# A graph network on one core: two middle biases moved from TensorE to VectorE, score rows carried through memory, leak by two exponentials, new queue orders

## Reference

```python
h = jnp.maximum(_layernorm(x), 0.0);  x = x + L0(h, adj)   # hypergraph convolution, 256 -> 512 -> 256
h = jnp.maximum(_layernorm(x), 0.0);  x = x + L1(h, adj)   # tanh(norm(A) @ h @ W + b)
h = jnp.maximum(_layernorm(x), 0.0);  x = x + L2(h, adj)   # attention, below
h = jnp.maximum(_layernorm(x), 0.0);  x = x + L3(h, adj)   # three graph layers, two with relu
# L2:
y = x @ w;  s = y @ a
A = s[..., :, None] + s[..., None, :]
A = jnp.tanh(A / 8.0) * 8.0
A = jnp.where(A >= 0, A, 0.1 * A)
A = jnp.exp(A) * A_shape
A = A / jnp.sum(A, axis=-1, keepdims=True) * jnp.sum(A_shape, axis=-1, keepdims=True)
out = A @ x @ w
# L3, twice with relu and once without:
x = jax.nn.relu(jnp.einsum('bnm,bmh->bnh', adj, x @ W1) + b1)
```

## Time and profile before

| | before |
|---|---|
| time, median of 3 runs | 1438.51 us (1437.08 to 1438.55) |
| the profiled execution | 1435.79 us, span of its trace 1433.8 us |
| TensorE busy | 1392.3 us, 97%, x10900 |
| TensorE weight loads | 1331.7 us, 93% |
| VectorE busy | 1287.9 us, 90%, x4001 |
| ScalarE busy | 990.5 us, 69% |
| GpSimd busy | 947.7 us, 66% |
| DMA | 62.70 MB, mean 44 GB/s |

### The profile page before, as it was taken

How to read it: one execution, slowest core, us unless ns; L and a number is a source line. 1 busy time by engine, 2 the same in 40 slices (tenths; PEclk the granted TensorE clock), 3 DMA queues, 4 the chain that set the end, 5 groups by cost and what they waited for, 6 DMA issues and landing times.

```text
span 1433.8 us, 34585 instructions
## 1 busy us (share of the span) xinstructions
PE 1392.3 (97%) x10900; PEld 1331.7 (93%) x10900; DVE 1287.9 (90%) x4001; ACT 990.5 (69%) x2312; POOL 947.7 (66%) x1876
## 2 busy tenths in 40 slices
PE   3799999999999999999999999999999999999997
PEld 2799999999999999999999999999999999999996
DVE  5789999999999999999999999999999999999984
ACT  3577777777777777777777777777777777777763
...
DMA packets 83078, 62.70 MB, mean 44 GB/s; under 512 B 40304, under 2 KB 65520, under 8 KB 83056
## 3 DMA queue, kind: packets, MB, share of 16 engines
...
...
## 4 chain that ended last, share of the span: by engine, by line
PE 95%; DVE 2%; ACT 1%; issue 0%; DMA 0%; POOL 0%; SPq 0%; DVEq 0%; POOLq 0%
PE BANK L365 29%; PE BANK L330 24%; PE BANK L372 15%; PE WIDE L365 8%; PE WIDE L341 8%; PE WIDE L372 4%; PE BANK L357 2%; PE BANK L315 2%; PE BANK L384 2%; DMA TMP_D<-in_l2wt 0%; PE WIDE L278 0%; DVE BN_B L550 0%; DVE BN_C L550 0%; ACT UHI_D L444 0%; PE WIDE L284 0%
## 5 line engine op out<-in xcount | busy, mean ns | idle before, releaser
L444 ACT ACTIVATE UHI_B<-BANK 128x512 fp32r<-128x512 f32 x96 | 57.0, 593 | 43.9 <-PE BANK L330 43.9
L444 ACT ACTIVATE UHI_D<-BANK 128x512 fp32r<-128x512 f32 x96 | 57.1, 595 | 41.1 <-PE BANK L330 41.1
L444 ACT ACTIVATE UHI_C<-BANK 128x512 fp32r<-128x512 f32 x96 | 57.0, 594 | 41.0 <-PE BANK L330 41.0
L444 ACT ACTIVATE UHI_A<-BANK 128x512 fp32r<-128x512 f32 x96 | 57.1, 594 | 39.1 <-PE BANK L330 39.1
L599 DVE TENSOR_TENSOR ULO_D<-BANK,UHI_D 128x512 fp32r<-128x512 f32 x96 | 65.2, 680 | 18.7 <-ACT UHI_D L444 18.0
L732 POOL TENSOR_TENSOR LN_A<-MV_A,EPS 128x2 f32<-128x2 f32 x80 | 15.9, 198 | 92.3 <-DVE MV_A L558 92.3
L599 DVE TENSOR_TENSOR ULO_A<-BANK,UHI_A 128x512 fp32r<-128x512 f32 x96 | 65.2, 680 | 12.3 <-ACT UHI_A L444 11.8
L599 DVE TENSOR_TENSOR ULO_C<-BANK,UHI_C 128x512 fp32r<-128x512 f32 x96 | 65.1, 678 | 11.1 <-ACT UHI_C L444 9.3
L599 DVE TENSOR_TENSOR ULO_B<-BANK,UHI_B 128x512 fp32r<-128x512 f32 x96 | 65.7, 684 | 10.4 <-ACT UHI_B L444 8.5
L732 POOL TENSOR_TENSOR LN_D<-MV_D,EPS 128x2 f32<-128x2 f32 x80 | 15.8, 197 | 84.7 <-DVE MV_D L558 84.7
L732 POOL TENSOR_TENSOR LN_B<-MV_B,EPS 128x2 f32<-128x2 f32 x80 | 16.7, 209 | 78.2 <-DVE MV_B L558 78.2
(11 more groups left out here) (500 smaller groups left out, 6009.6 us busy)
## 6 DMA issues: line engine op xcount, KB each, us to landing
X_A<-in_xs SPq DMA_DIRECT2D x16, 256.0 KB, 2.8
X_B<-in_xs SPq DMA_DIRECT2D x16, 256.0 KB, 2.8
X_C<-in_xs SPq DMA_DIRECT2D x16, 256.0 KB, 2.8
X_D<-in_xs SPq DMA_DIRECT2D x16, 256.0 KB, 2.8
out_rows<-O_A SPq DMA_DIRECT2D x16, 256.0 KB, 2.0
out_rows<-O_B SPq DMA_DIRECT2D x16, 256.0 KB, 2.1
out_rows<-O_C SPq DMA_DIRECT2D x16, 256.0 KB, 2.1
out_rows<-O_D SPq DMA_DIRECT2D x16, 256.0 KB, 2.1
```

The costliest lines, as they stand in the source:

```text
L444: nc.scalar.activation(UHI[s][:, 0:J * D], bank(s, step)[:, :], ACT.Copy).then_inc(sem(f"c{step}"), 1)
```

## The change

Six parts. (1) The bias matmuls of 4W and 5W are gone. VectorE adds the bias, reading the bank and writing H (`biased`, steps 4W and 5W of DVE_SLOTS); ScalarE's `relu` then works on H in place. The bank is free when VectorE is through. (2) `scores_high`, `scores_low` and the four matmuls are gone. SP writes the two score columns to a row buffer in memory, waits until they have landed, and reads them back spread over all partitions into AE (`spread_scores` in the SP block, step S). Step 3S stays in TensorE's table as a turn on a bank, without an instruction. (3) `scores_tanh` works on AE in place. ScalarE then takes exp(8 t) into the bank and exp(0.8 t) into AE, and VectorE's `leak` takes the greater of the two. (4) The maxima with immediates become tensor_tensor instructions with constant tiles ONE and LEAST. (5) `shifts` goes behind A's 0W, and the splitting of the weights is spread over the first pass. (6) All five tables have other numbers.

```diff
-    "G": 5.35, "0U": 12.31, "0W": 15.06, "1U": 28.24, "1W": 29.30, "2U": 37.53, "2W": 47.58, "3S": 58.05,
...
+    "G": 1.24, "0U": 4.10, "0W": 11.16, "1U": 24.70, "1W": 25.19, "2U": 35.53, "2W": 42.62, "3S": 53.06,
...
-    "F": -62.50, "W": -31.17, "X": -29.19, "D": -22.11, "R": -19.11, "T": 2.34, "O": 88.50}
+    "F": -83.35, "D": -79.48, "W": -50.53, "X": -36.90, "R": -17.35, "T": -0.50, "S": 30.01, "O": 88.50}
...
-        BIAS = {step: sb(f"BIAS{step}", [P, J, D], F32R) for step in ("4W", "5W")}
-        SHARES = sb("SHARES", [P, P], F32R)
+        BIAS = {"4W": L3B1, "5W": L3B2}
...
+        ROWS = nc.dram_tensor("score_rows", [len(STREAMS), J, P], F32).ap()
...
+            def spread_scores(s, group, n):
+                i = STREAMS.index(s)
+                done = 16 * group + 16
+                done = done if isinstance(group, int) else sp.snap(done)
+                sp.wait_ge(sem("s_ready"), n)
+                sp.dma_start(ROWS[i].rearrange("j p -> p j").unsqueeze(2), ST[s][:, SC, :].unsqueeze(2), allow_slow_non_contiguous=True)\
+                    .then_inc(sem("scores_out", s), 16)
+                sp.wait_ge(sem("scores_out", s), done)
+                sp.dma_start(AE[s][:, :, :], ROWS[i].partition_broadcast(P)).then_inc(sem("scores_in", s), 16)
...
-                    biased = step in BIAS
-                    if biased:
-                        nc.tensor.matmul(to[:, :], SHARES[:, :], BIAS[step][:, :, :], start=True, stop=False)
...
-            def spread_scores(s, c, k):
-                pe.wait_ge(sem("scores_split"), c["n1"])
-                bank_free(s, "3S", k)
-                for j in range(J):
-                    for part in (SHI, SLO):
-                        last = nc.tensor.matmul(bank(s, "3S")[:, j * P:(j + 1) * P], part[s][:, j:j + 1].to_broadcast([P, P]),
-                                                IDENTR[:, :], start=(part is SHI), stop=(part is SLO))
-                last.then_inc(sem("p3S"), 1)
...
+            run(pe, PE_ORDER, parts, {("A", "0W"): shifts, last_free: lambda: pe.wait_ge(sem("w2c_ready"), 1)})
...
-                act.wait_ge(sem("p3S"), c["n1"])
-                for j in range(J):
-                    last = nc.scalar.activation(AE[s][:, j, :], bank(s, "3S")[:, j * P:(j + 1) * P], ACT.Tanh,
+                act.wait_ge(sem("scores_in", s), c["dma"])
+                for j in range(J):
+                    last = nc.scalar.activation(AE[s][:, j, :], AE[s][:, j, :], ACT.Tanh,
...
-                act.wait_ge(sem("scores_leak"), c["n1"])
-                to = bank(s, "3S")[:, 0:J * P]
-                nc.scalar.activation(to, to, ACT.Exp, scale=8.0).then_inc(sem("e_ready"), 1)
+                act.wait_ge(sem("scores_tanh"), c["n1"])
+                bank_free(act, s, "3S", k, [x[2] for x in ACT_ORDER if x[:2] == (s, "3E")][0])
+                nc.scalar.activation(bank(s, "3S")[:, 0:J * P], AE[s][:, :, :], ACT.Exp, scale=8.0)
+                nc.scalar.activation(AE[s][:, :, :], AE[s][:, :, :], ACT.Exp, scale=8.0 * LEAK).then_inc(sem("both_exp"), 1)
...
-                    act.wait_ge(sem(f"p{step}"), c["n1"])
-                    nc.scalar.activation(H[s][:, :, :], bank(s, step)[:, :], ACT.Relu).then_inc(sem(f"c{step}"), 1)
+                    act.wait_ge(sem(f"b{step}"), c["n1"])
+                    nc.scalar.activation(H[s][:, :, :], H[s][:, :, :], ACT.Relu).then_inc(sem(f"c{step}"), 1)
...
-                nc.vector.tensor_scalar(ST[s][:, CNM, :], ST[s][:, CNT, :], 1.0, None, ALU.max).then_inc(sem("cnm"), 1)
+                nc.vector.tensor_tensor(ST[s][:, CNM, :], ST[s][:, CNT, :], ONE[:, :], ALU.max).then_inc(sem("cnm"), 1)
...
-                nc.vector.tensor_scalar(ST[s][:, DNM, :], DNS[s], TINY, None, ALU.max).then_inc(sem("dnm"), 1)
+                nc.vector.tensor_tensor(ST[s][:, DNM, :], DNS[s], LEAST[:, :], ALU.max).then_inc(sem("dnm"), 1)
...
+            def biased(step):
+                def f(s, c, k):
+                    dve.wait_ge(sem(f"p{step}"), c["n1"])
+                    rows = bank(s, step)[:, :].rearrange("p (j d) -> p j d", j=J)
+                    nc.vector.tensor_tensor(H[s][:, :, :], rows, pair(BIAS[step][:, :]), ALU.add).then_inc(sem(f"b{step}"), 1)
+                return f
...
-            def scores_high(s, c, k):
-                dve.wait_ge(sem("s_ready"), c["n1"])
-                nc.vector.tensor_copy(SHI[s][:, :], ST[s][:, SC, :]).then_inc(sem("s_high"), 1)
-            def scores_low(s, c, k):
-                dve.wait_ge(sem("s_high"), c["n1"])
-                nc.vector.tensor_tensor(SLO[s][:, :], ST[s][:, SC, :], SHI[s][:, :].bitcast(F32), ALU.subtract)\
-                    .then_inc(sem("scores_split"), 1)
...
-                dve.wait_ge(sem("scores_tanh"), c["n1"])
-                nc.vector.scalar_tensor_tensor(bank(s, "3S")[:, 0:J * P], AE[s][:, :, :], LEAK, AE[s][:, :, :], ALU.mult,
-                                               ALU.max).then_inc(sem("scores_leak"), 1)
+                dve.wait_ge(sem("both_exp"), c["n1"])
+                to = bank(s, "3S")[:, 0:J * P]
+                nc.vector.tensor_tensor(to, to, AE[s][:, :, :], ALU.max).then_inc(sem("e_ready"), 1)
...
-            dve.wait_ge(sem("ones_ready"), 1)
-            run(dve, DVE_ORDER, parts, {("A", "TB"): first_weights, ("A", "0U"): centred_weights, ("A", "0S"): last_weights})
+                     "3A": aggregate("3"), "4W": biased("4W"), "5W": biased("5W"), "6W": last_out, **{step: low(step) for step in U_STEPS}, "1U": low_hidden}
+            dve.wait_ge(sem("ones_ready"), 2)
+            run(dve, DVE_ORDER, parts, {
+                ("A", "TB"): lambda: low_weights("0W"), ("A", "DD"): spread_vectors, ("A", "0W"): centred_weights,
+                ("A", "0A"): lambda: low_weights("1W"), ("A", "1U"): lambda: low_weights("2W"),
+                ("A", "1A"): lambda: low_weights("3W"), ("A", "2U"): lambda: low_weights("4W"),
+                ("A", "2W"): lambda: low_weights("5W"), ("A", "2A"): lambda: low_weights("6W")})
...
```

More of the change, by code:

```diff
@@ L89, in program @@
         IDENT = sb("IDENT", [P, P])
-        IDENTR = sb("IDENTR", [P, P], F32R)
         OFFDIAG = sb("OFFDIAG", [P, P])
@@ L365, in f @@
                                 nc.tensor.matmul(dst, UHI[s][:, at[m]:at[m] + P], w[:, m, :],
-                                                 start=(w is lo and m == 0 and not biased), stop=False)
+                                                 start=(w is lo and m == 0), stop=False)
                         if step == "1W":
@@ L396, in _ @@
                 **{step: weigh(step) for step in W_STEPS}}
-            run(pe, PE_ORDER, parts, {("A", "0U"): shifts, ("A", "0W"): lambda: pe.wait_ge(sem("shifts_ready"), 1)})
+            first = [x[:2] for x in PE_ORDER if not x[2]]
+            last_free = first[[n for n, x in enumerate(first) if x[1] in WIDE_STEPS][1] - 1]
+            run(pe, PE_ORDER, parts, {("A", "0W"): shifts, last_free: lambda: pe.wait_ge(sem("w2c_ready"), 1)})
         @block.scalar
```

111 lines of the change are left out of this document (49 added, 62 removed), and 16 rows, old and new, of tables (ACT_SLOTS, DVE_SLOTS).

## The result

The changed kernel took 2039.06 us (median of 4 runs, 2038.31 to 2042.42) against 1437.88 us (1437.08 to 1438.55) of the kernel before on the same chip: 1.419 times as long, 95% interval 1.416 to 1.421. The forecast was 1385 with a range to 1422. The wait that the rival "slower" describes came, and far larger than that rival priced it.

A forecast was written before the change was run, and what follows sets the result against it. TensorE's own work was taken to bound the passes. From 1435.8 us, -56 (matmuls removed), -6 (start), +3 (tail) and +6 (lock) gave 1382.8, or 1385 at the median's level; own range 1372 to 1397, wider range 1368 to 1422.

The forecast's parts named there:

- the rival "slower": The scores' detour through memory sets the pace; 1487 us with a read of 4 us; chance 0.10.
- the price of the write: SP's write of 256 single score values to memory: taken to land in 2.5 us.
- r: Length of the scores' detour (write, read, two hand-overs): 5.1 us, ends 4.3 and 10.4.
- The read: SP's spread read of the scores into AE: 2.3 us, far end 7.9.
- The path and its room: From A's 6U to D's 2U: 9.1 us beside TensorE's 10.1 of other work, leaving 1.0 before the lock.
- the small lock: GpSimd's RH holds up VectorE's second score instruction by up to 1.2 us; TensorE stands 0.1 a quarter, +6 us.
- Removed from TensorE: Spreading and bias matmuls gone: 0.94 us less in each group, counted for 60 groups, -56 us.
- VectorE: Its work a quarter goes from 20.1 to 18.7 to 19.8 us, under TensorE's 20.55, so not the bound.
- the rival on the lock: GpSimd additions hold up VectorE's small maxima and score instructions, 0.3 to 0.8 us a quarter; 1409 us; chance 0.24.
- 128x2 maximum: VectorE's small maximum, 1294 ns before: whether it falls to about 150 left open, 0 to 1.15 us a group.
- Start: Spreading VectorE's weight splitting lets A's 1U begin earlier than 37.20 us: -6 us (0 to -9).
- Tail: The last group's chain is longer by two adds and the detour, less cast, difference and matmuls: +3 us (1 to 6).

The follow-up runs named there:

- p6: Changed kernel, scores left out: values written to adjacent words of a buffer nothing reads, AE loaded from a bias row; 1997.13 us, executed once.
- p4: Changed kernel, scores left out: values written 64 bytes apart in a buffer nothing reads, AE loaded from a bias row; 1422.16 us, executed once.
- p8: p4 with ScalarE's 4U at 94.31 instead of 94.32 in its table, which removes the tie with 0U; 1394.51 us, ratio 0.9716.
- e4: Changed kernel with the scores turned by VectorE before the write, 8 pieces of 128 bytes instead of 256 of 4; 1457.05 us, ratio 1.0107.
- e3: Changed kernel with two scores written side by side, 128 pieces of 8 bytes instead of 256 of 4; 1607.03 us, ratio 1.115.
- p3: Changed kernel, scores left out: values written 512 bytes apart in a buffer nothing reads, AE loaded from a bias row; 1416.11 us, executed once.
- e6: e4 with VectorE's 6U at 103.08 instead of 105.76 and ScalarE's 4U at 94.31 instead of 94.32; 1429.78 us, ratio 0.9958.
- e11: e8 with GpSimd's addition RH behind its small score instruction instead of ahead of it; 1381.79 us, ratio 0.9583.
- e10: e8 with VectorE's 0U at 22.50 instead of 23.74 and GpSimd's RH behind its small score instruction; 1411.95 us, ratio 0.9817.
- e8: e6 with VectorE's 4U at 84.85 instead of 86.54, ahead of the graph convolution output's statistics; 1419.98 us, ratio 0.9895.

## Why the prediction was wrong, step by step

- **The step that failed** is the price of the write: "For the write I bound by the store of a stream, 2.0, and DIAG, 256 single values read, 2.5." It landed in 7.7 us. Both rows were of the wrong kind. DIAG reads single values that lie far apart in memory and writes them into partitions; the store writes 2 KB in one piece for each partition. What the row of scores has, and neither of them, is many pieces written side by side into memory, sixteen in 64 bytes. Shown: p6 against p4, one distance changed, 1997 against 1422 us. With the detour short and the tie of the orders (below) out, p8 takes 1394.5 us, at the edge of the forecast's own range of 1372 to 1397. The range's upper end of r, 10.4, held the far end of the read but no far end of the write; it should have had one, since no row showed the thing.
- **The read**, taken at 2.3, landed in 4.9 to 5.1, and in 2.9 once the write was fast (e4). That the spread read is slow by itself, on which the rival "slower" hung, is not so. Why it takes 5 us behind the slow write is open: p6, with the slow write and another source, has 2.9 in three streams and 4.9 in one, and in the changed kernel the loads and stores behind it are late as well, so it is not a matter of this read alone.
- **The path and its room** were right. "TensorE stands r - 5.0 us in each quarter": 12.5 - 5.0 = 7.5, measured 7.3; in e3 6.9 - 5.0 = 1.9, measured 2.0. With r at 1.6 + 3.1 + 0.3 = 5.0 (p3) it stands no more. So was the small lock: in the passes the second score instruction is 1.51 us beside RH's 1.28.
- **What the formula left out** is TensorE's clock: 2.35 us more a quarter at the low level, for 7.3 of gap. The rival "slower" at r = 12.5 would give 1379 + 60 x 7.5 = 1829; with 60 x 2.35 of clock it is 1970. Of the 69 us that remain, the tie of the next point is 19. TensorE stood 63 times and not 60, by estimate 3 x (7.5 + 2.35) = 30 more, and the 6 of the start were not gained; the last 14 were not told apart.
- **The orders** were taken at no cost beyond the lock. They cost 1.2 us a pass by the tie, 19 us by the wait and 16.5 by e6. The prediction walked one quarter through the queues; the tie is in another one, and a list of the four streams side by side would have shown it beforehand.
- **Removed from TensorE**, -0.94 us a quarter: in e11 a quarter is 20.38 against 21.49, -1.11. The size is right, but the rows don't show that the whole 1.11 is the removed work: before the change one quarter (from 1W of B at 740.42 to 1W of C at 761.39) takes 20.97 us and the next (to 783.09) 21.70, with no wait listed. And it is all there only when TensorE waits for nothing; with the lock on and waits of 0.2 to 0.6 us, half of it or more went again.
- **VectorE**: "it does not become the bound by its sum, but it has 1 to 2 us of air". Its sum was indeed not the bound (81.2 of 85 us in e11), and its lateness was what e4 to e10 fought with, as the rival on the lock (1397 to 1427, chance 0.24) says. Its price, 60 x 0.5 = 30 us, was somewhat low: e8 and e6 lie 45 and 54 us above e11 by the ratios. In the changed kernel VectorE's quarter is 81.18 / 127 x 30.7 = 19.6 us of busy time, near the 19.8 that the rule on the lock gave. That it is near is chance: the 128x2 maximum, on which 19.8 or 18.7 hung, did fall (next point), which alone gives the 18.7; but the two score instructions, 0.42 each before, now take 0.94 in the mean, 1.0 us more a quarter, which is not in that sum. The prediction had this lock in its path and left it out of VectorE's sum.
- **128x2 maximum**: 0.14 us in all streams (1.29 for A before). I had left open between 0 and 1.15. Its place changed: before, it began at 707.54 with a GpSimd addition of 1.29 us that began at 707.53; now it runs at 955.05, where GpSimd is between two small instructions (one ends at 955.03, the next begins at 955.11). Whether the form alone would have freed it wasn't tried. The exponential leak is 0.43 (0.41 taken). The groups of C in the changed kernel:

```profile
L567 DVE TENSOR_TENSOR ST_C<-G_C,LEAST 128x2 f32<-128x2 f32 x16 | 2.3, 144 | 0.0
L558 DVE TENSOR_TENSOR ST_C<-ST_C,ONE 128x2 f32<-128x2 f32 x16 | 2.2, 137 | 0.0
L641 DVE TENSOR_TENSOR BANK<-BANK,AE_C 128x256 f32<-128x256 f32 x16 | 6.9, 432 | 126.3 <-ACT AE_C L482 126.3
```

- **Start**, -6 us: A's 1U begins at 37.44, not earlier than before. Wrong by 6. The lump on VectorE is gone as expected: although it waits for TensorE's weight products until 27.38, it closes A's statistics at 32.6, 3 us earlier than before (35.43 and 0.24). But GpSimd, which works them into the norm, comes to them only at 35.88. The two additions that it had behind it by 29.04 before now come at 30.57 and 34.66, since the first waits for ScalarE, and ScalarE for what VectorE makes of the weight products. The prediction looked at VectorE's share of this chain alone. VectorE:

```profile
27.38 0.42 DVE L525 COPY BW<-WIDE 128x256 f32<-128x256 f32 x1 [4.26 <-PE WIDE L320]
...
30.95 1.28 DVE L538 BATCH_NORM_STATS2 BN_A<-Z_A 128x6 f32<-128x512 f32 x2 [1.49 <-ACT Z_A L456]
32.34 0.25 DVE L546 BATCH_NORM_AGGREGATE MV_A<-BN_A 128x2 f32<-128x6 f32 x2
```

GpSimd:

```profile
34.66 1.26 POOL L760 TENSOR_TENSOR RES_A<-RES_A,B 128x512 f32<-128x512 f32 x1
35.88 0.20 POOL L723 TENSOR_TENSOR LN_A<-MV_A,EPS 128x2 f32<-128x2 f32 x1
```

- **Tail**, +3 us: not measured by itself.

So the mechanism by which the change was to gain is real (e11, with the scores turned and four places in the tables changed, ends 3 us under the forecast, 7 by the ratio), and the same change as it was written cost 600, because its smallest transfer was priced by transfers that differ from it in the one thing that mattered.
